# Low-rank products of the down and the second feed-forward weights as full 128-row float32r contractions

## What is computed

```
w = NF4[codes] * scales
q, k, v = _lin_lora(x, W_q/k/v, ...);  attn = (q + k + v) / 3;  x1 = x + _lin_lora(attn, W_o, ...)
h = silu(_lin_lora(x1, W_gate, ...)) * _lin_lora(x1, W_up, ...)
d = h @ W_down.T + (h @ A_down.T) @ B_down.T          # rank 16
x = layernorm(x + x1 + d)
x = layernorm(x + x @ W_ffn.T + (x @ A_f.T) @ B_f.T * 0.25)     # rank 64
x = layernorm(x + attention(x));  x = layernorm(x + experts(x))
```

## Time and profile before

| | |
|---|---|
| median of three runs | 570.43 us |
| span of the profiled execution | 569.6 us |
| TensorE matmul, busy | 506.0 us (89%) |
| DVE busy | 434.0 us (76%) |
| ACT busy | 362.1 us (64%) |
| POOL busy | 335.2 us (59%) |

### The profile page before, as it was taken

One profiled execution on the slowest core, in us unless ns is written; L12 is line 12 of the kernel. 1 busy time (PEld: TensorE's weight loads), 2 busy tenths in 40 slices (PEclk: granted clock), 3 DMA queues, 4 the chain that ended last, 5 costly groups with the idle time before them and its releaser, 6 DMA issues.

```text
span 569.6 us, 8051 instructions
## 1 busy us (share of the span) xinstructions
PE 506.0 (89%) x2260; PEld 398.3 (70%) x2260; DVE 434.0 (76%) x821; ACT 362.1 (64%) x655; POOL 335.2 (59%) x318
## 2 busy tenths in 40 slices
PE   0465549988999999999999999989999799999995
PEld 0142338766788878777777787768888588888874
DVE  7899988999857779989899899257745885465542
ACT  8899956698757668878789686216768542232121
POOL 5889824179857678979879789314739811020011
PEclk9986659999999999999999999999999999999999
DMA  8732402033323122323323230064000000010011
GB/s 249 256 100 86 129 18 67 13 99 119 100 69 93 56 93 96 107 82 112 106 91 108 80 112 20 1 249 148 2 0 2 0 2 1 18 39 20 0 37 38
DMA packets 20379, 42.97 MB, mean 75 GB/s; under 512 B 3312, under 2 KB 3440, under 8 KB 19824
## 3 DMA queue, kind: packets, MB, share of 16 engines
q1 hardware_dynamic: 20112, 42.09, 23.1%
q0 software_dynamic: 224, 0.38, 0.3%
HBM read 40.36 MB, written 2.10 MB: 75 GB/s over the span
## 4 chain that ended last, share of the span: by engine, by line
PE 68%; POOL 15%; issue 13%; ACT 2%; DVE 2%; POOLq 0%; ACTq 0%; DVEq 0%
PE bank L870 58%; POOL wf L615 6%; PE bank L1002 3%; POOL wf L623 3%; POOL wf L628 2%; PE bank L961 2%; POOL wf L634 2%; PE bank L987 1%; PE bank L1106 1%; PE bank L888 1%; PE bank L895 1%; ACT prob L831 1%; ACT pT_hi L681 0%; PE bank L889 0%; DVE rmax L1312 0%
## 5 line engine op out<-in xcount | busy, mean ns | idle before, releaser
L702 ACT ACTIVATE bank<-code 128x512 f32<-128x512 int32 x372 | 207.8, 595 | 25.1 <-DVE half L1165 12.1
L615 POOL TENSOR_TENSOR wf<-halves 128x512 f32<-128x512 f32 x62 | 80.1, 1292 | 78.5 <-DVE halves L1169 77.3
L870 PE MATMUL bank<-x_hi,gu_hi 128*128 128x512 f32 x224 | 89.5, 399 | 2.7 <-POOL gu_lo L641 2.7
L664 POOL TENSOR_TENSOR rstd<-veps,neg_half 128x1 f32<-128x1 f32 x32 | 17.6, 549 | 121.7 <-issue 110.5
L870 PE MATMUL bank<-x_lo,gu_hi 128*128 128x512 f32 x224 | 87.3, 390 | 0.0
L870 PE MATMUL bank<-x_hi,gu_lo 128*128 128x512 f32 x224 | 87.3, 390 | 0.0
L1165 DVE SCALAR_TENSOR_TENSOR half<-half,bank 128x512 f32<-128x512 f32 x124 | 81.5, 680 | 3.6 <-ACT bank L702 3.6
L1163 DVE SCALAR_TENSOR_TENSOR half<-code,bank 128x512 f32<-128x512 int32 x124 | 79.2, 680 | 6.5 <-ACT bank L702 5.1
L1169 DVE TENSOR_TENSOR halves<-half,bank 128x512 f32<-128x512 f32 x124 | 79.3, 680 | 0.0
L623 POOL TENSOR_TENSOR wf<-wf,scale 128x512 f32<-128x512 f32 x50 | 65.3, 1305 | 3.9
L870 PEld LDWEIGHTS bank<-x_hi,gu_hi 128*128 128x128 f32 x224 | 42.1, 188 | 16.6 <-issue 6.3
(11 more groups left out here) (195 smaller groups left out, 1133.7 us busy)
## 6 DMA issues: line engine op xcount, KB each, us to landing
code<-codes SPq DMA_DIRECT2D x62, 256.0 KB, 2.7
scale<-scales SPq DMA_DIRECT2D x100, 128.0 KB, 2.9
xs<-xT SPq DMA_DIRECT2D x1, 2048.0 KB, 12.9
ea_raw<-ex_A SPq DMA_DIRECT2D x1, 2048.0 KB, 9.6
eb_raw<-ex_B SPq DMA_DIRECT2D x1, 2048.0 KB, 7.7
out<-rows SPq DMA_DIRECT2D x8, 256.0 KB, 2.0
bgu_raw<-loB_gu SPq DMA_DIRECT2D x1, 1792.0 KB, 10.5
wqkv_raw<-w_qkv SPq DMA_DIRECT2D x1, 768.0 KB, 4.0
```

What stands on the lines that cost most here:

```text
L615: pool.tensor_tensor(w, halves[:, j % 2, 0, :], halves[:, j % 2, 1, :], ALU.subtract).then_inc(diff_done, 1)
L664: pool.tensor_tensor(rstd[:, s:s + 1], veps[:, s:s + 1], neg_half[:, :], ALU.pow)\
L702: nc.scalar.activation(plane[m % RING_PLANE][:, :], src, func, bias=float(start), scale=float(slope)).then_inc(plane_ready, 1)
L870: last = nc.tensor.matmul(ps, a, b, start=start and i == 0 and n == 0, stop=stop and i == len(terms) - 1 and n == 2)
```

## The change

- The factors of `down` are laid out in two groups of 64 rows. In group g stand three copies of A's half g (rows of A for chunks 7g to 7g + 6) and of B, 16 rows each, and 16 rows of zeros. `la_dp` becomes A high, A low, A high; `lb_dp` becomes B high, B high, B low, with the other group's rows zero. One 128-row matmul gives the three products of a chunk (line 904 of the changed kernel).
- The factors of the second feed-forward weight are stored twice, over 128 rows. `la_fp` is A high over A low, `lb_fh` and `lb_fl` are B's high and low parts in both halves; two 128-row float32r matmuls take the place of the float32 one (lines 914 to 916).
- `dprep` works on wider tiles: `la_d` 128x896 for 128x512, `lb_d` 128x1024 for 128x512. A new item `("fprep", 0)` stands at the start of block f = 4: two copies of 128x512 on ACT, a scalar_tensor_tensor and a tensor_tensor of 128x512 on DVE.
- Four loads are larger: `la_d` 448 KB and `lb_d` 512 KB for 256 KB each, `la_f` and `lb_f` 256 KB each for 128 KB. Tiles are placed anew in SBUF: `la_d` shares its place with `act_f`, so the first silu on ACT also waits for `dprep_done`.

```diff
@@ vector_order
+        if f == 4:
+            order.append(("fprep", 0))
@@ ACT
                     copy(la_dp[:, :], la_d[:, :], dprep_hi)
-                    copy(lb_dh[:, :], lb_d[:, :], dprep_hi)
+                    copy(lb_dhi[:, :, :], lb_d[:, :, :], dprep_hi)
+                elif kind == "fprep":
+                    act.wait_ge(loraf_in, 32)
+                    act.wait_ge(p_ready, NB)
+                    copy(la_fhi[:, :], la_f[:, :], fprep_hi)
+                    copy(lb_fh[:, :], lb_f[:, :], fprep_hi)
...
+                    if n == 0:
+                        act.wait_ge(dprep_done, 1)
@@ TensorE, lora
                     pe.wait_ge(dprep_done, 2)
-                    r, cut = 32 * (k // 4), slice((k % 4) * P, (k % 4 + 1) * P)
-                    nc.tensor.matmul(lora_ps[:, :], la_dp[r:r + 32, cut], lb_dh[r:r + 32, :], start=True, stop=False)
-                    nc.tensor.matmul(lora_ps[:, :], la_dp[r:r + RANK, cut], lb_dl[r:r + RANK, :],
-                                     start=False, stop=True).then_inc(lora_ready, 1)
+                    g, cut = k // (NF // 2), k % (NF // 2)
+                    nc.tensor.matmul(lora_ps[:, :], la_dp[:, cut * P:(cut + 1) * P], lb_dp[:, g, :],
+                                     start=True, stop=True).then_inc(lora_ready, 1)
                     return
                 else:
-                    pe.wait_ge(loraf_in, 32)
-                    a, b = la_f[:, k * P:(k + 1) * P], lb_f[:, :]
+                    pe.wait_ge(fprep_done, 2)
+                    a = la_fp[:, k * P:(k + 1) * P]
+                    nc.tensor.matmul(lora_ps[:, :], a, lb_fh[:, :], start=True, stop=False)
+                    nc.tensor.matmul(lora_ps[:, :], a, lb_fl[:, :], start=False, stop=True).then_inc(lora_ready, 1)
+                    return
@@ DVE
                     nc.vector.scalar_tensor_tensor(la_dp[:, :], la_dp[:, :].bitcast(F32), low_rows[:, 1:2],
                                                    la_d[:, :], ALU.mult, ALU.add).then_inc(dprep_done, 1)
-                    dve.wait_ge(p_ready, NB)
-                    low(lb_dl[:, :], lb_d[:, :], lb_dh[:, :], dprep_done)
+                    nc.vector.scalar_tensor_tensor(lb_dp[:, :, :], lb_dhi[:, :, :].bitcast(F32), low_rows[:, 2:3],
+                                                   lb_d[:, :, :], ALU.mult, ALU.add).then_inc(dprep_done, 1)
+                elif kind == "fprep":
+                    dve.wait_ge(fprep_hi, 2)
+                    nc.vector.scalar_tensor_tensor(la_fp[:, :], la_fhi[:, :].bitcast(F32), low_rows[:, 3:4],
+                                                   la_f[:, :], ALU.mult, ALU.add).then_inc(fprep_done, 1)
+                    low(lb_fl[:, :], lb_f[:, :], lb_fh[:, :], fprep_done)
```

More of the change, by code:

```diff
@@ L247, in tail_order, with build @@
     return [(kind, *map(int, args.split("."))) for kind, args in items]
-def build(nc, codes, scales, scales_qkv, eye, down_low, xT, loA_o, loB_o, loA_qkv, loB_qkv, loA_gu, loB_gu,
+def build(nc, codes, scales, scales_qkv, eye, stack_low, xT, loA_o, loB_o, loA_qkv, loB_qkv, loA_gu, loB_gu,
           loA_d, loB_d, loA_f, loB_f, w_qkv, b_qkv, w_o, b_o, ex_A, ex_B, w_r, out):
@@ L258, in build @@
         neg_half = ctx.enter_context(nc.sbuf_tensor("neg_half", [P, 1], F32))
-        low_rows = ctx.enter_context(nc.sbuf_tensor("low_rows", [P, 2], F32))
+        low_rows = ctx.enter_context(nc.sbuf_tensor("low_rows", [P, 4], F32))
         warm = ctx.enter_context(nc.sbuf_tensor("warm", [P, 1], F32))
@@ L304, in build @@
         bu4 = at("bu4", 194, [P, FF], F32R)
[L305 to L309, removed]
+        la_d = at("la_d", 30, [P, FF // 2])
+        la_dp = at("la_dp", 94, [P, FF // 2], F32R)
+        lb_d = at("lb_d", 201, [P, 2, 512])
+        lb_dp = at("lb_dp", 201, [P, 2, 512], F32R)
+        lb_dhi = at("lb_dhi", 82, [P, 2, 512], F32R)
         a4_lo = at("a4_lo", 132, [P, KT, P], F32R)
         ident = at("ident", 207, [P, P])
-        la_f = at("la_f", 90, [FFN_RANK, 512])
-        lb_f = at("lb_f", 92, [FFN_RANK, 512])
+        la_f = at("la_f", 90, [P, 512])
+        la_fp = at("la_fp", 90, [P, 512], F32R)
+        la_fhi = at("la_fhi", 86, [P, 512], F32R)
+        lb_f = at("lb_f", 92, [P, 512])
+        lb_fh = at("lb_fh", 205, [P, 512], F32R)
+        lb_fl = at("lb_fl", 92, [P, 512], F32R)
         wff_hi = at("wff_hi", 34, [P, KT, H], F32R)
@@ L413, in build @@
         dprep_done = sem("dprep_done")
+        fprep_hi = sem("fprep_hi")
+        fprep_done = sem("fprep_done")
         p_ready = sem("p_ready")
@@ L555, in _ @@
                     sp.dma_start(la_d[:, :], loA_d).then_inc(lorad_in, 16)
-                    sp.dma_start(lb_d[:, :], loB_d).then_inc(lorad_in, 16)
-                    sp.dma_start(low_rows[:, 1:2], down_low).then_inc(lorad_in, 16)
+                    sp.dma_start(lb_d[:, :, :], loB_d).then_inc(lorad_in, 16)
+                    sp.dma_start(low_rows[:, 1:4], stack_low).then_inc(lorad_in, 16)
                 if c == ("g", 3):
@@ L1423, in laid_out @@
     zero = np.zeros((RANK, FF), np.float32)
[L1424 to L1430, removed]
+    la_d = np.zeros((P, FF // 2), np.float32)
+    lb_d = np.zeros((P, 2, 512), np.float32)
+    stack_low = np.zeros((P, 3), np.float32)
+    for g in range(2):
+        for i in range(3):
+            r = 64 * g + RANK * i
+            la_d[r:r + RANK] = Ad[:, g * FF // 2:(g + 1) * FF // 2]
+            lb_d[r:r + RANK, g] = Bd.T
+            stack_low[r:r + RANK, :2] = (-float(i == 1), -float(i == 2))
+    stack_low[FFN_RANK:, 2] = -1.0
     A4 = np.tile(np.concatenate([Ah[4], Ah[5]]), (4, 1))
@@ L1437, in laid_out @@
         eye=np.eye(P, dtype=np.float32),
-        down_low=np.where(np.arange(P) % 32 < RANK, 0, -1).astype(np.float32)[:, None], xT=tiles(x.T),
+        stack_low=stack_low, xT=tiles(x.T),
         loA_o=Ah[3], loB_o=Ba[3].T, loA_qkv=Ah[:3].reshape(3 * RANK, H),
@@ L1441, in laid_out @@
         loA_gu=tiles(A4.T), loB_gu=np.stack(B4, 1), loA_d=la_d, loB_d=lb_d,
-        loA_f=np.asarray(a["L0_ffn_lora_A"]), loB_f=np.asarray(a["L0_ffn_lora_B"]).T,
+        loA_f=np.tile(np.asarray(a["L0_ffn_lora_A"]), (2, 1)),
+        loB_f=np.tile(np.asarray(a["L0_ffn_lora_B"]).T, (2, 1)),
         w_qkv=tiles(np.asarray(a["L1_attn_Wqkv"])),
```

## The result

| | before | after |
|---|---|---|
| median | 570.76 us (570.41 to 571.95, 4 runs) | 562.8 us (561.32 to 564.97, 4 runs) |
| ratio, 95% interval | | 0.986 (0.983 to 0.989) |
| span of the profiled execution | 569.6 us | 559.5 us |
| time of that execution | not recorded | 561.32 us |
| TensorE / DVE, busy | 506.0 / 434.0 us | 495.7 / 437.1 us |

The forecast (faster, 560.9 us, range 559.7 to 563.4) was right in sign, and the range holds the time. A second set of runs of the changed kernel gave 561.75 us (561.17 to 562.8, 5 runs) against 571.67 us (570.05 to 574.85, 9 runs), ratio 0.983 (0.980 to 0.986). So the gain is 8 to 10 us, and runs of one program lie up to 4 or 5 us apart. In the first set the two runs of the changed kernel with a mean granted clock of 0.966 and 0.965 took 561.3 and 561.8 us, the two with 0.960 took 563.8 and 565.0; the profiled one is the fastest.

A forecast was written before the change was run, and what follows sets the result against it. POOL was taken to bound the kernel from 119.46 to 146.82 us, then TensorE's row of matmuls. Span 569.6 - 10.5 (TensorE) + 0.95 (`dprep`) = 560.05 us, plus 0.8 to the median: 560.9 us, range 559.7 to 563.4.

The forecast's parts named there:

- TensorE's row: TensorE's matmuls behind 146.82 us: down chunks give 7.3 us, second feed-forward chunks 3.2, together 10.5 us off.
- `dprep`: DVE's wider instructions before POOL's stretch: `halves` come 0.95 us later, all on the path; bounds 0.75 to 1.45.
- its slack is POOL's stretch: TensorE waits some 0.9 us longer for `dprep_done`; POOL bounds that stretch, so this costs no second microsecond.
- the first rival: DVE becomes the bound in the blocks with eight halves: 561.5 to 562.8, say 562.3 us; chance 0.18.
- the sum: Forecast span: 569.6 - 10.5 + 0.95 = 560.05 us; the median was put 0.8 us above it.
- DVE does not become the bound: Over two repeating blocks TensorE needs 35.4 us, DVE 35.2, so TensorE stays the bound by 0.2 us.
- its soft place: Hand-over of a gate chunk's low part from POOL to TensorE: 0.17 us of room stays, no stall taken.
- `fprep`: DVE's two instructions behind the add at 185.30 us: at most some 2.3 us, within 2.73 us idle, costing nothing.
- the excess was not from the narrow rows: Rival on TensorE's products: bank entry or waits cause the excess, so only 4.0 us gained, 566.5 us; chance 0.08.
- `dprep` is hidden: Rival: POOL's stretch has unseen room, so the 0.95 us stays away, 559.9 us; chance 0.08.
- Slower: Rival: DVE's lag makes each down unit a round trip; needs over 38.1 us DVE work per two blocks; chance 0.02.
- no change: Rival: the same DVE round-trip mechanism, losing exactly 2.7 us for each pair of blocks; chance 0.02.

The follow-up runs named there:

- the down-only kernel: The changed kernel with the second feed-forward chunks' float32 matmul of before and no `fprep`; 565.8 us, ratio 0.990.
- the last one: The changed kernel without the low-rank matmul of each gate and up unit from block 2 on; 557.02 us, one run.
- the third experiment: The changed kernel with each down chunk's product over its own group's 64 rows instead of all 128; 567.81 us, ratio 0.992.

## Why the prediction was right, step by step

**TensorE's row: right.** 7.3 us for the down chunks and 3.2 for the feed-forward ones made 10.5; the stretch lost 10.21. The price of a product, 0.227 us, and the 0.81 us of a feed-forward chunk stand in the rows above as predicted. Blocks without a feed-forward chunk give 0.66 us each ahead of block 6, as predicted (from one down product to the next 18.11 us before, 17.45 after). Two blocks with a feed-forward chunk give 37.52 - 35.48 = 2.04 us instead of 2.13, and this 0.09, three to four times, is the missing 0.3 us. Most of it is a wait that the prediction did not name. In these blocks the down product needs bank 3, and it has to wait until DVE's merge of the other chunk is done with it. The weight load of the product shows it, in three blocks alike:

```profile
246.28 0.19 PEld L904 LDWEIGHTS bank<-lb_dp,la_dp 128*128 128x128 f32 x1 [0.21 <-DVE wf L1205]
```

The load begins 0.21 us late, but the next matmul only 0.06 us; the other 0.03 us of each pair of blocks stay open.

**`dprep`: right in sum, its two parts less so.** 0.95 us predicted, 1.00 measured, and the same 1.00 in every kernel with the wide tiles and `dprep` in its place. ACT's `lb_dhi` took 1.05 us, as in the working, and DVE starts 0.04 us behind it, as reckoned. From start to start DVE's two took 1.12 and 1.31 us, against 1.02 + 0.2 and 1.16: 0.10 too much and 0.15 too little, which nearly cancel by luck. The excess of the second is not explained. POOL's `gu_lo` ended at 114.57, 0.25 us into `la_dp`. By the rule of the Trainium skill that the prediction weighed (SBUF — State Buffer, on the shared port pair) DVE would wait that long. The 1.0 us worked out from it is what was measured, but this does not bear it out, since the overlapped instruction shows an excess of 0.10 us and not 0.25.

**The step that failed: "its slack is POOL's stretch".** The longer wait for `dprep_done` was to cost nothing. It holds in the down-only kernel, with the same gap and 27.03 us, and in the last one, with 27.05. In both traces of the changed kernel the lower clock followed, and 0.9 us were lost. The cover was there for a delayed TensorE; it wasn't there for a TensorE at half speed, since ACT and DVE also take their next steps from it.

**The 1.9 us between forecast and median.** By the number alone the first rival did better: its 562.3 us (561.5 to 562.8) is nearer to 562.8 than the forecast of 560.9 (560.3 to 561.5), and only the range as a whole held the time. The rows decide against that rival. TensorE's stretch is 212.96 us with 212.81 busy, and two blocks take 35.48 us in which TensorE is never idle. The 1.9 us come from elsewhere: the median lies 1.5 us above the profiled run, the offset between span and time is 1.8 us instead of 0.8, and the span is 0.55 us shorter than the sum.

**The offset between span and time.** The sum's 560.05 us of span stand against 559.5 and 559.4 measured. The prediction then added 0.8 us, the distance of the median of before from the span of its one trace. The four runs of the changed kernel have a time 1.8 us above their own span, each time (561.32 over 559.5, 564.97 over 563.2). By that offset the trace of before was of an execution of about 571.4 us (an estimate), above its median. So the close agreement of the spans is partly luck: 560.05 - 1.75 (the earlier first cut) + 0.89 (the clock) + 0.05 (`dprep`) + 0.29 (TensorE's row) makes the 559.5 measured.

**DVE does not become the bound: right, with more room than said.** Before, two blocks took 37.52 us; I predicted 35.4 and they take 35.48. DVE's adds of one down unit, two blocks apart:

```profile
242.23 0.69 DVE L1270 TENSOR_TENSOR rows<-bank,rows 128x512 f32<-128x512 f32 x1 [0.60 <-PE bank L886]
...
277.72 0.69 DVE L1270 TENSOR_TENSOR rows<-bank,rows 128x512 f32<-128x512 f32 x1 [0.40 <-PE bank L886]
```

One wait of 0.4 us is left in two blocks where there were 0.26 and 2.03. The prediction said 0.2. The hand-over of the gate chunk, its soft place, cost nothing visible.

**`fprep`: nothing, as said, but with less to spare.** Its two steps on DVE and the next add:

```profile
184.79 1.19 DVE L1247 SCALAR_TENSOR_TENSOR la_fp<-la_fhi,low_rows,la_f 128x512 fp32r<-128x512 f32 x1
185.91 1.77 DVE L1164 TENSOR_TENSOR lb_fl<-lb_f,lb_fh 128x512 fp32r<-128x512 f32 x1
...
189.40 0.69 DVE L1267 COPY rows<-bank 128x512 f32<-128x512 f32 x1
```

They take 2.8 us, from 184.79 to the next start at 187.61, not at most 2.3, and the add of 189.40 us has no wait left, where before it had 2.73. "The next add still waits" was wrong; that TensorE shows no gap there was right.

**The other rivals.** That the excess was not from the narrow rows fell with the third experiment; that `dprep` is hidden, with the 8.06 us. *Slower* and *no change* needed DVE as the bound, which it is not.

## What to carry to other kernels

A narrow matmul of 512 columns in a row of full ones cost nearly three times the step of a full one, so zeros that fill a contraction to 128 rows were cheaper than saving them. Where an engine's wait is covered by another's work, ask also what it costs if the clock falls there: here the wait was free and the fall was not. Compare traces by stretches between common events, since here the first 110 us alone differed by up to 2.8 us between traces. Preparation that stands on the path was worth moving to an engine with true gaps; moved along its own engine, beside POOL's steps, it was paid again.

## What was not expected of the hardware

- One 64-row float32r matmul among 128-row ones costs 0.64 us (0.227 + 0.41), a pair of 32 and 16 rows 0.88 (0.227 + 0.66): the first narrow one bears most of it, and the second adds one step. A load of 64 rows is as short as one of 128 (0.18 and 0.19 us), but it isn't begun ahead of its matmul.
- A POOL add of 128x1024 took 4.21 us while DVE worked on two SBUF operands for 1.92 us of it; the one of 128x896 without such company took 2.13, which makes an estimate of 2.4 for 1024 columns. The 1.8 us above it are nearly the whole overlap: POOL got next to nothing done beside DVE. DVE's 128x512 subtract with `fprep` took 1.77 us beside POOL's steps, where one of that size from PSUM takes 0.69, and POOL's 1.73 instead of 1.29:

```profile
98.25 2.53 DVE L1247 SCALAR_TENSOR_TENSOR bg<-bg,low_rows,bgu_raw 128x1792 fp32r<-128x1792 f32 x1 [0.30 <-ACT bg L699]
...
98.86 4.21 POOL L654 TENSOR_TENSOR lb_dp<-lb_dneg,lb_d 128x1024 fp32r<-128x1024 f32 x1
...
107.02 2.13 POOL L658 TENSOR_TENSOR la_dp<-la_dneg,la_d 128x896 fp32r<-128x896 f32 x1 [3.95 <-PE bank L897]
```

- Kernels that are the same up to there, with the same idle 2.9 us on TensorE, lose 1 us behind it in some traces and nothing in others, by whether the granted clock falls to its lower level there.
